# Roll layer of a two-layer fusion model: where TensorE runs unread products, and how 32 images are split into groups

## What is computed

```python
z = softmax(einsum('bse,he->bsh', x, W_A) * SCALING, axis=1)
roll = transpose(z)[:, :, (i - j) % S] * tril
v = einsum('bse,fe->bsf', x, W_V).reshape(B, S, H, D)
out = einsum('bhij,bjhd->bihd', roll, v).reshape(B, S, E)
return einsum('bse,fe->bsf', out, W_O) + b_O
```

## Time and profile before

| | us |
|---|---|
| Three runs | 1059.83, 1064.62, 1065.32 |
| Their median | 1064.62 |
| Profiled execution, its own time | 1058.96 |
| Its span, first to last instruction | 1057.2 |

### The profile page before, as it was taken

One profiled execution on the slowest core, in us unless ns is written; L12 is line 12 of the kernel. 1 busy time (PEld: TensorE's weight loads), 2 busy tenths in 40 slices (PEclk: granted clock), 3 DMA queues, 4 the chain that ended last, 5 costly groups with the idle time before them and its releaser, 6 DMA issues. The chain is left out here.

```text
span 1057.2 us, 29755 instructions
## 1 busy us (share of the span) xinstructions
PE 950.0 (90%) x10428; PEld 746.9 (71%) x10459; DVE 582.8 (55%) x1446; ACT 413.2 (39%) x1102; POOL 519.2 (49%) x714
## 2 busy tenths in 40 slices
PE   8899999998747999999999997689999957999996
PEld 6667777777634888888888875355556635888895
DVE  1778888865994777433333325677886452111111
ACT  2267677734243343343443422223333222332431
POOL 0055665620604777777777627777772002333432
PEclk9999999999969999999999998899999987999998
DMA  7010000002004988877788723334455047476750
GB/s 257 1 46 2 0 0 0 2 11 75 1 1 156 307 276 260 273 245 223 243 265 254 229 89 100 105 112 124 125 140 220 22 159 251 142 255 230 266 156 25
DMA packets 79821, 149.30 MB, mean 141 GB/s; under 512 B 18892, under 2 KB 53327, under 8 KB 75760
## 3 DMA queue, kind: packets, MB, share of 16 engines
q1 hardware_dynamic: 34768, 77.15, 21.5%
q0 software_dynamic: 17712, 47.88, 15.7%
q10 hardware_dynamic: 27248, 23.09, 6.5%
HBM read 200.22 MB, written 31.73 MB: 219 GB/s over the span
## 5 line engine op out<-in xcount | busy, mean ns | idle before, releaser
L1332 POOL DMA_INDIRECT x_x<-m_x_rows,x_idx x170 | 165.7, 975 | 74.7 <-issue 36.1
L1358 PE MATMUL x_pup<-x_xt,x_w 128*128 128x128 f32 (+1 forms) x2176 | 182.9, 250 | 0.0
L1358 PEld LDWEIGHTS x_pup<-x_xt,x_w 128*128 128x128 f32 (+1 forms) x2176 | 166.9, 165 | 5.9 <-issue 5.7
L1623 POOL DMA_INDIRECT rl_y<-m_y_rows,rl_idx x136 | 132.7, 976 | 43.6 <-issue 38.1
L1439 DVE TENSOR_TENSOR x_hid<-x_gate,x_pup 128x128 f32<-128x128 f32 x170 | 48.9, 287 | 147.9 <-ACT x_gate L1411 141.1
L1372 PE MATMUL x_pdown<-x_w,x_hid 128*128 128x256 f32 (+1 forms) x408 | 104.2, 389 | 0.2 <-DVE x_y L1446 0.2
L1407 ACT ACTIVATE x_xt<-x_pturn 128x256 f32<-128x256 f32 x170 | 65.2, 383 | 89.1 <-PE x_pturn L1343 86.4
L442 POOL TENSOR_TENSOR wa_probs<-wa_probs,wa_peak 68x544 f32<-68x544 f32 x64 | 69.9, 1092 | 57.6 <-DVE wa_peak L593 54.9
L2405 DVE TENSOR_TENSOR x_y<-x_pdown,x_b 128x256 f32<-128x256 f32 x21 | 8.9, 424 | 149.2 <-PE x_pdown L2359 149.2
L2391 ACT ACTIVATE x_hid<-x_pup,x_b 128x128 f32<-128x128 f32 (+1 forms) x200 | 52.6, 356 | 93.1 <-PE x_pup L2342 92.9
L1411 ACT ACTIVATE x_gate<-x_pup 128x128 f32<-128x128 f32 x170 | 47.1, 277 | 92.5 <-PE x_pup L1358 91.8
(11 more groups left out here) (345 smaller groups left out, 1917.9 us busy)
## 6 DMA issues: line engine op xcount, KB each, us to landing
x_w<-in_experts SPq DMA_DIRECT2D x204, 384.0 KB
late_w<-in_w SPq DMA_DIRECT2D x28, 1024.0 KB, 12.5
m_y_rows<-x_y ACTq DMA_DIRECT2D x170, 128.0 KB
xT<-in_w SPq DMA_DIRECT2D x12, 1024.0 KB, 7.0
xn<-in_w SPq DMA_DIRECT2D x10, 1024.0 KB, 11.5
h<-in_w SPq DMA_DIRECT2D x10, 1024.0 KB, 15.3
m_x_rows<-xn SPq DMA_DIRECT2D x34, 128.0 KB, 1.9
x_x<-m_x_rows,x_idx POOLq DMA_INDIRECT x170
```

Of the source, the lines that this page charges most:

```text
L1332: nc.gpsimd.indirect_dma_start(x[:, s, :], None, x_rows, bass.IndirectOffsetOnAxis(ap=idx[:, s:s + 1], axis=0))\
L1358: mm = nc.tensor.matmul(pup[rows:rows + wide, bank, m * P + side * wide:m * P + (side + 1) * wide], w[:, lane, first:first + wide], xt[:, ...
L1623: nc.gpsimd.indirect_dma_start(y[:, t % YR, kk, :], None, y_rows, bass.IndirectOffsetOnAxis(ap=idx[:, n:n + 1], axis=0))\
```

## The change

```diff
-    SIZES = [2] + [4] * 7 + [2]
+    SIZES = [2] + [4] * 6 + [2] * 3
@@ SyncE
-                    if g == NG - 4:
+                    if g == 4:
@@ TensorE
+                def steady(g):
+                    return 1 < g < NG - 1
+
                 def fill_values(g, n):
+                    if steady(g):
+                        return
@@
                 def fill_mid(g, n):
+                    if steady(g):
+                        return
@@
+                    if has1:
+                        fill(g1, 6 * SIZES[g1] // GI if steady(g1) else 20 if g1 < 2 else 4)
                     for t in tiles_in(g1):
                         turn("in", t)
-                        fill(g1, 1)
+                        if not steady(g1):
+                            fill(g1, 1)
                     if has1:
-                        fill(g1, 1)
                         mix_logits(g1)
                         values(g1, 0)
@@
                     if has2 and not has1:
-                        fill(g2 + 1, 8)
+                        fill(g2 + 1, 5)
```

## The result

The changed kernel takes 1087.55 us (median of three runs, 1086.78 to 1088.67) against 1064.62 before; the ratio is 1.0243, with a 95% interval of 1.0204 to 1.0282. It is 2.4% slower, outside the range that was given and on the side that was given 0.13. The profiled execution took 1087.55 us, with a span of 1085.8 against 1057.2: 28.6 us more.

A forecast was written before the change was run, and what follows sets the result against it. Gathers set the pace up to 696.4, TensorE after; steady steps fall from 22.19 to 21.6 us. Step 8's start plus the tail gave logits at 861.5 against 861.34, middle 0.3 us earlier; forecast 1062.0 us, range 1056 to 1069.

The forecast's parts named there:

- the side that was given 0.13: Whole kernel: the outcome slower, chance 0.13, most of it from rival B; faster had 0.25, no change 0.62.
- The six: Unread products put behind the forwards, ahead of a steady step's first turn in: nothing covers them, 1.3 us paid in full.
- the removed products: 17 unread products taken out of a steady step: 3.7 us of issue, of which 1.93 us comes back.
- rival B: Steady steps: small unfilled waits make the clock fall, about 1.27 us each, 6 to 10 us over five to eight steps; chance 0.15.
- a stretch at 250 to 260 us: Argument against a clock fall: TensorE busy 7.53 of 10 us there was granted 1.00; a steady step would be busy 87%.
- The tail: End of the roll layer, longer by a step: what the steady steps give, the extra step takes; logits at 861.5 against 861.34.
- step 8: First step with a group of 2 coming in: 17.3 us, beginning at 803.5, or 802.6 with the clock kept.
- step 9: Step with a group of 2 in both places: TensorE's share 13.5 us, VectorE's chain longer, 13.9 us taken.
- step 10 on: One pair and one tile out: 11.8 us to its forwards, then 15.0 us to the logits.
- rival C: Tail worse than read: steps 9 and 10 each 2 us longer, the time 3 to 4 us longer; chance 0.17.
- The weights: Four loads a step earlier: gathers at most 4.5 us later, covered up to 3.9, costing at most 0.6; 0 taken.
- Step 3: Begins at 696.4, set by gathers; its earlier clock fall cost 1.27 us, and the change gains nothing or that 1.27.

The follow-up runs named there:

- e8: Changed kernel with the old nine groups, weight loads back at `NG - 4` and no unread products in steady steps; 1057.67 us, ratio 0.9968.
- e1: Kernel before with only the change's groups and weights at group 4, all unread products where they were before; 1066.46 us, ratio 1.0045.
- e3: Changed kernel with a steady step's six products moved from ahead of the first turn: four behind the first invert, two behind the second; 1078.34 us, ratio 1.0162.
- e5: e3 with the four weight loads issued at group 5 instead of 4; 1069.24 us, ratio 1.0088.
- e12: Changed kernel with the six (three) products ahead of the first turn taken out of the steady steps; 1072.26 us, ratio 1.0111.
- e9: e8 with the weight loads at group 6, behind the last gather; 1056.25 us, ratio 0.9941.
- e6: e3 with the old nine groups and the weight loads at group 5; 1063.15 us, ratio 1.0003.
- e7: e3 with the old nine groups and the weight loads at group 6; 1057.08 us, ratio 0.9965.
- e11: e7 with three more unread products in front of each full step; 1054.90 us, ratio 0.9954.
- e2: Changed kernel with the old nine groups and weight loads back at `NG - 4`, keeping the new placing of products; 1071.28 us, ratio 1.0096.

## Why the prediction was wrong

**The work in a step was right.** The six paid in full, 1.93 us back from the removed products, 21.6 us a step: the clean step 6 took 21.44, and without the six 20.1 to 20.2 (e8), where the same walk gives 22.19 - 1.93 = 20.3. The removed products did cover waits for the copies.

**The clock was given to the wrong case: rival B.** The forecast let all steady steps run at 1.00 and put the clock at nothing in its sum. The step that failed is the reason for that, "Against: a stretch at 250 to 260 us with TensorE busy 7.53 of 10 us was granted 1.00 ..., and a steady step would be busy 87%". Busy share did not decide: step 6 of the changed kernel was busy 19.10 of 21.44 us (89%) and kept the clock, step 5 as full of work lost it. The rival named the right waits, "between and behind the inverts", with 0.15.

**B's price was about a third of the true one.** It was "about 1.27 us" a fall, from a fall in step 3 before that hit turns and first products. That one lasted 3.4 us (696.8 to 700.2), so it cost 0.37 us for each us of its length. Here a fall lasts 6.8 to 10.3 us over inverts and projection and costs 24.43 - 21.44 = 3.0 to 25.96 - 21.44 = 4.5 us, which is 0.44 for each us. So most of the difference is the length of the falls, the rest their place. Rival B with 3 to 4.5 us over its five to eight steps would have given 15 to 36 us, and the 24.9 measured lie within.

**The tail.** I gave step 8 17.3, step 9 13.9, step 10 on 11.8 + 15.0 = 26.8; measured 21.32, 19.27, 26.38. With the products kept (e1) they take 18.04, 17.82 and 26.15, so of the 12.8 us lost here 7.8 belong to the groups and 5.0 to the missing products. The term furthest off is step 9: in e1 TensorE waits 0.49 and 0.44 us ahead of the turns out, and the clock falls (833.8 to 840.6) even with the products. Step 8 was right but for the clock: 17.3 without a fall, against 18.04 with all products and none. This is what rival C named, and by e1 it is smaller than B.

**The weights.** "The delay ... costs at most 0.6; I take 0" was right for the changed kernel, whose steps had grown by the falls: no combine from step 4 on waited for its gather there. With steps of 22.2 us (e1) tile 13's combine waited 3.78 us and TensorE's step was no longer for it, as the cover of 3.9 us had it. With steps of 20.7 us the bound did not hold: the combine waited 6.20 us (e3), and 1.00 with the loads elsewhere (e5), about 5 us of delay against the 4.5 read from another stage. Step 6 grew by 3.9 us, and a fall began at the turn behind the wait. What orders the cases is how early the first load is issued against the last of the gather's eight DMAs: 5.2 us before it in e3 (766.81 against 771.97), 2.3 before it in e1 (768.60 against 770.94), and 0.5 behind it in e12 (769.19 against 768.71), where the combine waited for nothing even with steps of 20.1 us.

**Step 3.** I let it lose its fall or keep it (0 to 1.27 us). Its fall at the turns went, and a longer one came at the inverts: 24.91 us at 0.86, with a wait of the second invert for VectorE's terms (tile 6's combine, at 701.52, had waited 1.65 us for its gather).

## What to carry to other kernels

Unread products can be worth more by their place than by their number: in the full steps profiled, six among the thinnest matmuls held the clock where six in one run ahead of the step did not, with steps of 20.7 against 21.4 us. That is no rule on number: with none at all (e8, e9) the kernel was as fast. Where a kernel has a thin stretch with nothing in it, one clean step in a profile proves little: look at the granted clock of every repetition, and of several executions, before products are moved or taken out. And when steps get shorter, ask which transfer loses its slack first; moving a bulk load behind the last gather was worth 6 us here (e6 against e7). The best versions found, e9 (0.9941), e11 (0.9954) and e7 (0.9965), have the old groups, at most nine products a step instead of 17, and the loads at group 6; their intervals overlap.

## What the runs showed of the hardware

- The clock fell in a step in which TensorE waited nowhere longer than 0.59 us and was busy 23.57 of 25.96 us (step 5 of the changed kernel).
- The same instruction stretch kept or lost its clock from one step to the next (changed kernel: step 5 lost it, step 6 kept it, after the same 12.01 us). Leaving the products of the full steps out was 13.6 us faster than six in one run ahead of the first turn (e8 against e2).
- A gather of 1 MB in eight indirect DMAs landed about 5 us late beside 4 MB of weight loads (e3 against e5: 6.20 us of wait against 1.00), while GpSimd went on issuing one every 1.25 us. The combine began 7.77 us behind the last of the eight in e3, and 2.73 in e5. In e12, where the loads were issued 0.5 us behind that last one, it did not wait.
